# TensorE's background items of a fused convolution, attention and feed-forward stage, put at other steps of their quads

## The chip, the cores and the metric

The kernel runs on one core of one Trainium2 chip. The metric is the device time in microseconds (us). A core has four compute engines with a queue of instructions each: TensorE (PE in the profile; its weight loads are PEld), VectorE (DVE), ScalarE (ACT) and GpSimd (POOL); SyncE (SP) issues DMAs. Engines wait for one another by semaphores. TensorE writes PSUM, eight banks of 2 KB a partition, and the others read it.

## The reference

Four images of 128 channels and 64x64 pixels go through a group norm and a 3x3 deformable convolution (layer 0), then as 4096 tokens an image through attention and two feed-forward parts (layer 1). Cut to what matters:

```
x = x + deform_conv(group_norm(x))                 # 9 taps, bilinear corners gathered by offset
t = tokens(x)
q = ring(layer_norm(t).reshape(.., 16 heads, 8) + theta)     # products of cosines
attn = softmax(q q^T / sqrt(8)) q                  # 1024 tokens by 1024, 16 heads, 8 wide
x1 = ln(t_n + attn @ w_comb.T + b)
t = t + ln(x1 + relu(cos(x1[:8]) cos(ry) @ w1.T + b1) @ w2.T + b2)
t = t + experts(layer_norm(t))                     # gate logits, softmax over tokens, top 8 of them
```

The attention takes the tokens of an image as one sequence of 4096 here (the reference's shapes follow from its input), with the scores symmetric in the two token indices.

## The kernel before

The program has four stages: offsets, the convolution of the first image, a main stage (`stage_main`), and experts. The change is in the main stage alone.

**Quads and steps.** The main stage works on 16 quads, a quad being four heads of one image (`QUADRUPLES`, numbered 0 to 15 here). A quad has 8 units of 512 query tokens, and 304 steps (`Plan.steps`). A step is three slabs of 128 by 512 scores. For each step k TensorE computes the scores (L1157, three matmuls), ScalarE takes the exponential of 128x1536 numbers at once (L1255), and later TensorE multiplies the result with the values, a group of four heads at a time (L1189, 8 records of 512 columns). Because scores are symmetric, one part of the exponentials is kept (`e_kept`), turned by 16 DMAs and four VectorE transposes (L1140, L1151) and used as `e_turned` (L1180, 16 records, a group too). 256 groups of values a quad, 32 a unit.

**TensorE's order.** `AttnStep.quad_pe` writes it out step by step (k from 2 to 305). In step k it waits until the exponential of step k - 2 is done, because there are two PSUM tiles of scores; issues the scores of step k; then so many value groups; then the background item that is placed at k, if there is one. How many groups:

```
at_once = total if over else 0 if k in background else 1
needed = max(background[k][0] if k in background else 0, plan.before.get(k - 1, 0))
... range(min(max(min(ready - done, at_once), ready - done - self.PV_BEHIND, needed - done), closed - done))
```

So a step has one group, or none where an item stands; but where more than `PV_BEHIND` = 2 ready groups wait, or where a buffer of exponentials has to come free (`plan.before`: ScalarE's exponential k waits for them), the groups are caught up in that step, item or not. Items placed at step 306 or later are issued one behind the other at the quad's end, ahead of the next quad's step 2.

**Background items.** They are the rest of TensorE's work, in a fixed order a quad. All use one PSUM bank (`Misc`): an item waits until VectorE has read the one before it, and VectorE's program has the readers in the same order. Their names in this text:
- F0 to F7: `finish_pe` of the unit before (4 transposes of `acc_sb`, L1114). VectorE's read of the accumulators (L1092) comes ahead of it, and the next unit's first value group waits for that read too.
- tap: one of three products of a tile of the later images' convolution (`taps_pe`, L731), copied out at L740.
- gT, gL: the gate's transpose and logits (`gate_pe`, L1405, L1407). gT waits for two layer norms of VectorE (`norms_dve`), which wait for a load of `t1`.
- ctxT, comb, zbT, w1a, w1b, w2a, w2b: the seven items of a feed-forward pair (`item_pe`, L1511 to L1527). zbT reads what VectorE makes of comb in `first_dve` (L1447 to L1460); w1a and w1b are read by a relu (L1484), w2a and w2b together at L1490.
- stn0a to stn3b: transposes of the next quad's queries (`stage_pe`, L1054).

**Kinds of quads.** "conv first" (quad 0) and "conv" (1 to 3) have taps and no feed-forward, "conv ffn taps" (4 to 6) both, "conv ffn" (7 to 11) the feed-forward and the convolution's sampling on VectorE, "ffn six", "ffn choice" and "ffn" (12, 13, 14) the feed-forward alone, "last" (15). `PLACES` holds the steps of the items, a tuple for each kind.

**VectorE** runs `conv_quad`, `last_pair` and `ffn_quad`, where the readers of the items stand between the sampling of gathered pixels (L779 to L794), the transposes (L1151), the reads (L1092) and the norms. Where an item comes late, VectorE waits, and all behind it.

Of the kernel before, what the change touches and what calls it, by code (L numbers as in the profile page):

```python
# [1576 lines left out]
def stage_main(nc, d, r, stack):  # L1577
# [24 lines left out]
              (QUADRUPLES - 1, QUADRUPLES, "last", ()))  # L1602
    PLACES = {
        "conv first": (
            2, 4, 5, 6, 7, 26, 27, 46, 48, 49, 51, 52, 57, 59, 65, 67, 83, 88, 91, 98, 103, 111, 113, 120, 127, 139, 158, 161, 167,
            171, 176, 177, 180, 183, 184, 188, 198, 209, 214, 233, 236, 239, 244, 245, 251, 254, 256, 260, 261, 278, 298, 299,
        ),
        "conv": (
            2, 6, 7, 10, 13, 27, 28, 46, 52, 66, 82, 86, 88, 91, 99, 112, 114, 120, 126, 144, 157, 160, 163, 172, 176, 179, 180, 184,
            188, 190, 197, 211, 216, 233, 236, 238, 239, 245, 251, 252, 256, 257, 261, 276, 296, 301,  # L1610
        ),
        "conv ffn taps": (
# [3 lines left out]
        ),  # L1616
        "conv ffn": (
            5, 25, 28, 46, 49, 51, 53, 55, 66, 72, 77, 78, 82, 85, 106, 109, 121, 124, 128, 129, 132, 144, 149, 154, 155, 156, 159,
            181, 185, 194, 197, 199, 202, 203, 215, 221, 222, 227, 228, 234, 254, 259, 263, 270, 276, 294, 296, 300, 302, 303, 310,
            315,  # L1620
        ),
        "ffn six": (
# [3 lines left out]
        ),  # L1626
        "ffn choice": (
# [3 lines left out]
        ),  # L1631
        "ffn": (
# [3 lines left out]
        ),  # L1636
        "last": (
# [4 lines left out]
        ),  # L1642
    }
    SEGMENTS, at_misc, at_ffn, at_tap = [], 2, 0, TILES
# [1082 lines left out]
def build(nc, arrays, stages=("offsets", "conv", "main", "experts"), kinds={}):  # L2727
    d = Views(nc, arrays, kinds)
    with ExitStack() as whole:
        kept = Kept(nc, whole)  # L2730
        with ExitStack() as body:
            r = Shared(nc, body, kept)
            with ExitStack() as front:
                r.idx = front.enter_context(nc.sbuf_tensor("idx", [P, IMAGES * TILES * TAPS], I32))
                if "offsets" in stages:
                    with ExitStack() as st:
                        stage_offsets(nc, d, r, st)
                if "conv" in stages:
                    with ExitStack() as st:
                        stage_conv_first(nc, d, r, st)  # L2740
            if "main" in stages:
                with ExitStack() as st:
                    stage_main(nc, d, r, st)
        if "experts" in stages:
            with ExitStack() as st:
                stage_experts(nc, d, kept, st)
# [11 lines left out]
```

## Time and profile before

| | us |
|---|---|
| three timed runs | 7758.5, 7771.48, 7775.35; median 7771.48 |
| profiled execution, span | 7878.3 |
| ScalarE's exponentials, first to last start in the profile | 780.4 to 7622.4 |

The profiled execution took 107 us more than the median of the timed runs. Its span is the time from the first to the last instruction. In the profile a quad is the stretch between two exponentials 304 apart; the first exponentials of quads 1 to 15 start at 1253.0, 1677.4, 2098.7, 2516.9, 2946.8, 3382.2, 3816.2, 4242.6, 4668.4, 5091.3, 5512.3, 5934.1, 6354.2, 6775.6 and 7188.8 us. Step k of quad q is found by counting exponentials (L1255) from there.

### The profile page before, as it was taken

The page shows a single profiled execution, that of the slowest core. Times are in us where ns is not written, and L with a number is a line of the kernel's source. Part 1 is how long each engine was busy: PE and PEld are TensorE (multiplying, and loading weights), DVE is VectorE, ACT ScalarE, POOL GpSimd, SP SyncE. Part 2 cuts the span into 40 slices and gives each one's busy share as a digit, 9 for nine tenths or more (in the row PEclk, how much of TensorE's full clock was granted, in tenths as well). Part 3 has the DMA queues.
Part 4 walks back from the last instruction along what each step waited for, and adds up shares of the span by engine and source line. Part 5 has one row for each costly group of instructions (what it writes and reads, how often), then busy time and mean ns, then how long its engine had stood idle before and what let it go on. Part 6 is the DMA issues. An engine that isn't in the chain of part 4 may idle for free. (4 is left out here: it accounts for less than half of the span.)

```text
span 7878.3 us, 154169 instructions
## 1 busy us (share of the span) xinstructions
PE 6921.9 (88%) x58691; PEld 1859.1 (24%) x58691; DVE 4954.8 (63%) x12688; ACT 6811.0 (86%) x5455; POOL 1244.3 (16%) x1165
## 2 busy tenths in 40 slices
PE   4555799999999999999999999999999999999987
PEld 1444121111121222222221212222222212222224
DVE  5566555555555777777676767777775545454763
ACT  1222799999999999999999999999999999999971
POOL 1553111111111112111221111121210000000000
PEclk8777899999999999999999999999999999999997
DMA  6776575757566556656564545554643333232338
GB/s 214 208 210 185 125 167 138 171 137 166 141 159 147 147 135 169 154 131 157 124 144 112 138 115 132 120 136 113 145 117 77 98 74 92 69 98 64 99 98 265
DMA packets 1744564, 1080.93 MB, mean 137 GB/s; under 512 B 347914, under 2 KB 1645632, under 8 KB 1742828
## 3 DMA queue, kind: packets, MB, share of 16 engines
q1 hardware_dynamic: 1650972, 767.00, 40.2%
q0 software_dynamic: 92880, 304.42, 13.9%
q8 instruction: 448, 7.34, 0.4%
q14 instruction: 264, 2.16, 0.1%
HBM read 410.43 MB, written 190.83 MB: 76 GB/s over the span
## 5 line engine op out<-in xcount | busy, mean ns | idle before, releaser
L1255 ACT ACTIVATE e<-sc 128x1536 f32<-128x1536 f32 x4192 | 5715.2, 1604 | 193.2 <-PE sc L1157 121.7
L1189 PE MATMUL acc<-e,v_cur 128*9 128x512 f32 x25152 | 3341.7, 599 | 45.5 <-DVE acc_sb L1092 44.4
L1157 PE MATMUL sc<-b_unit,a_cur 32*128 32x512 f16 x14592 | 1916.7, 388 | 358.3 <-ACT e L1255 277.2
L1157 PEld LDWEIGHTS sc<-b_unit,a_cur 32*128 32x128 f16 x14592 | 472.6, 91 | 3826.3 <-ACT e L1255 2890.3
L1151 DVE STREAM_TRANSPOSE e_turned<-e_turned 128x1024 f32<-128x1024 f32 x896 | 1060.7, 1221 | 147.9 <-DMA e_turned<-e_kept 114.8
L1255 ACT ACTIVATE e_kept<-sc 128x1536 f32<-128x1536 f32 x672 | 960.6, 1567 | 63.0 <-PE sc L1157 32.1
L757 POOL DMA_INDIRECT room<-taps,idx_st x432 | 520.4, 1205 | 2109.0 <-ACT e L1255 890.2
L757 POOL DMA_INDIRECT corners<-taps,idx_st x441 | 435.1, 987 | 2052.3 <-ACT e L1255 1563.5
L1189 PE MATMUL acc<-e_kept,v_cur 128*9 128x512 f32 x4032 | 715.0, 611 | 0.0
L1189 PEld LDWEIGHTS acc<-e,v_cur 128*9 128x9 f32 x25152 | 394.3, 88 | 797.9 <-issue 730.8
L1180 PE MATMUL acc<-e_turned,v_cur 128*9 128x256 f32 x7168 | 472.2, 381 | 0.0
L621 ACT COPY cf_val_t<-cf_ps_t 128x512 f32<-128x512 f32 (+1 forms) x96 | 43.8, 481 | 407.1 <-PE cf_ps_t L661 260.9
L512 POOL DMA_INDIRECT cf_corners<-table,cf_idx x288 | 288.5, 1002 | 422.8 <-DVE cf_idx L537 160.9
L1092 DVE COPY acc_sb<-acc 128x512 f32<-128x512 f32 x129 | 88.8, 689 | 423.4 <-PE acc L1189 423.4
L740 DVE COPY conv_vals<-misc 128x384 f32<-128x384 f32 x192 | 106.7, 556 | 286.9 <-PE misc L731 247.9
L779 DVE TENSOR_TENSOR corners<-corners,w_st 128x1536 f32<-128x1536 f32 x144 | 250.0, 1755 | 9.0 <-DVE f_xn L103 5.9
L779 DVE TENSOR_TENSOR room<-room,w_st 128x1536 f32<-128x1536 f32 x144 | 248.3, 1747 | 2.9 <-DVE ctx_t L1105 2.7
L1043 DVE COPY b_all<-misc 128x1024 f16<-128x1024 f16 x64 | 44.3, 692 | 291.5 <-PE misc L1054 287.0
L649 PE MATMUL cf_ps_tap<-dcnw,cf_columns 128*128 128x384 f32 x192 | 86.6, 597 | 154.8 <-DMA cf_columns<-x_norm 154.8
L1180 PEld LDWEIGHTS acc<-e_turned,v_cur 128*9 128x9 f32 x7168 | 152.2, 90 | 197.4 <-issue 98.4
L551 DVE SCALAR_TENSOR_TENSOR cf_val<-cf_corners,cf_w,cf_val 128x128 f32<-128x128 f32 x576 | 157.7, 346 | 45.8 <-remote 20.7
L731 PE MATMUL misc<-dcnw,columns 128*128 128x384 f32 x384 | 178.2, 546 | 8.3 <-DVE f_gx_t L1390 4.2
(421 smaller groups left out, 5222.5 us busy)
## 6 DMA issues: line engine op xcount, KB each, us to landing
e_turned<-e_kept SPq DMA_DIRECT2D x3584, 128.0 KB
taps<-conv_vals SPq DMA_DIRECT2D x256, 288.0 KB
taps<-cf_tapped SPq DMA_DIRECT2D x128, 288.0 KB
ew<-in_ew SPq DMA_DIRECT2D x12, 1024.0 KB, 7.8
ew<-in_ew SPq DMA_DIRECT2D x48, 256.0 KB, 6.8
x_ch<-in_x SPq DMA_DIRECT2D x4, 2048.0 KB, 12.6
qn<-q SPq DMA_DIRECT2D x64, 128.0 KB
ctx<-ctx_t SPq DMA_DIRECT2D x128, 64.0 KB
```

The source lines that it names most:

```text
L512: pool.indirect_dma_start(corners[j][:, k, :], None, d.table, bass.IndirectOffsetOnAxis(idx_st[j][:, k:k + 1], 0)).then_inc(gathered[j], 16)
L551: last = v.scalar_tensor_tensor(out=dst, in0=src, scalar=wt, in1=dst, op0=ALU.mult, op1=ALU.add)
L731: m.pe_give(self.nc.tensor.matmul(m.bank[:, 0:3 * P], self.columns[j % 2][:], self.r.dcnw[:, 3 * g:3 * g + 3, :].rearrange("p k c -> p (k ...
L740: m.dve_give(self.nc.vector.tensor_copy(self.tapped[j % 2][:, 3 * P * g:3 * P * (g + 1)], m.bank[:, 0:3 * P]))
L757: pool.indirect_dma_start(self.corners[s][:, k, :], None, self.d.tap_tables[min(n, PAIRS - 1) * 2 // TILES - 1], bass.IndirectOffsetOnAxis ...
L779: last = v.tensor_tensor(g[:, taps], g[:, taps], w, ALU.mult)
L1092: self.nc.vector.tensor_copy(dst, src).then_inc(self.acc_read, 1)
L1151: self.nc.vector.transpose(x, x).then_inc(self.half_turned, 1)
L1157: last = self.nc.tensor.matmul(self.sc[k % self.SC][:, i, :], self.a[rows, t * P:(t + 1) * P], self.bst[u % 2][rows, :], start=True, stop= ...
L1180: last = self.nc.tensor.matmul(dst[:, :, half, :], self.v[:, plan.tiles_of[g][bo % 2], h, :], lines[:, :, :, h, 32 * bo:32 * bo + 32], sta ...
L1189: last = self.nc.tensor.matmul(self.acc[32 * h:32 * h + self.E1, :], self.v[:, t, h, :], src, start=(i == 0), stop=(i == self.UNIT - 1))
L1255: self.nc.scalar.activation(out, self.sc[k % self.SC][:], ACT.Exp, scale=1.0 / HD ** 0.5).then_inc(self.exp_done, 1)
```

## The change

`PLACES` has other steps for seven of the eight kinds; "last" keeps its own. The number of items and their order are the same, so every engine but TensorE has the same program, and TensorE has the same instructions in another order: an item comes some steps earlier or later between scores and value groups, and because a step with an item holds no group unless groups have to be caught up, value groups move as well. Of the kinds that the text speaks of most:

```
--- before.py
+++ after.py
@@ -1602,43 +1602,45 @@
     PLACES = {
...
         "conv": (
-            2, 6, 7, 10, 13, 27, 28, 46, 52, 66, 82, 86, 88, 91, 99, 112, 114, 120, 126, 144, 157, 160, 163, 172, 176, 179, 180, 184,
-            188, 190, 197, 211, 216, 233, 236, 238, 239, 245, 251, 252, 256, 257, 261, 276, 296, 301,
+            3, 5, 7, 9, 11, 19, 23, 46, 50, 55, 83, 85, 89, 91, 93, 101, 105, 121, 126, 131, 158, 160, 164, 166, 168, 170, 172,
+            183, 185, 188, 196, 207, 212, 233, 235, 239, 241, 243, 245, 247, 255, 257, 260, 270, 298, 300,
         ),
         "conv ffn taps": (
-            6, 9, 10, 13, 23, 26, 28, 32, 38, 46, 49, 51, 52, 54, 67, 72, 73, 76, 79, 85, 89, 94, 96, 106, 109, 111, 112, 115, 122,
-            126, 127, 129, 131, 142, 150, 153, 154, 156, 157, 162, 168, 169, 182, 183, 184, 187, 188, 195, 200, 202, 204, 206, 216,
-            222, 223, 228, 231, 233, 239, 243, 244, 254, 257, 258, 259, 260, 267, 271, 275, 294, 296, 300, 302, 303, 306, 311,
+            7, 12, 14, 16, 26, 28, 30, 31, 34, 46, 48, 51, 53, 55, 65, 71, 74, 76, 77, 84, 86, 94, 96, 108, 110, 112, 113, 116,
+            124, 126, 133, 135, 137, 145, 151, 153, 156, 157, 160, 162, 170, 172, 184, 186, 188, 189, 192, 200, 202, 210, 212,
+            214, 221, 227, 229, 232, 233, 235, 238, 246, 248, 259, 261, 263, 264, 266, 267, 272, 274, 300, 302, 304, 306, 307,
+            308, 309,
         ),
         "conv ffn": (
-            5, 25, 28, 46, 49, 51, 53, 55, 66, 72, 77, 78, 82, 85, 106, 109, 121, 124, 128, 129, 132, 144, 149, 154, 155, 156, 159,
-            181, 185, 194, 197, 199, 202, 203, 215, 221, 222, 227, 228, 234, 254, 259, 263, 270, 276, 294, 296, 300, 302, 303, 310,
-            315,
+            7, 26, 28, 46, 48, 51, 53, 55, 65, 71, 74, 76, 77, 84, 108, 110, 122, 125, 127, 129, 131, 141, 147, 150, 152, 153,
+            159, 184, 186, 198, 200, 203, 205, 207, 217, 223, 226, 228, 229, 234, 256, 258, 260, 270, 272, 293, 295, 297, 299,
+            301, 303, 304,
         ),
...
         "ffn choice": (
-            2, 10, 12, 15, 16, 25, 26, 31, 35, 38, 56, 74, 76, 84, 88, 91, 92, 94, 105, 107, 108, 109, 110, 121, 122, 129, 130, 131,
-            139, 140, 141, 146, 147, 155, 157, 159, 161, 167, 168, 169, 180, 182, 185, 186, 187, 195, 217, 230, 233, 237, 240, 241,
-            243, 252, 253, 255, 259, 264, 276, 294, 298,
+            3, 10, 14, 15, 16, 22, 23, 26, 28, 29, 46, 72, 74, 83, 85, 91, 92, 94, 103, 104, 107, 109, 110, 121, 123, 129, 130,
+            131, 138, 139, 142, 144, 145, 153, 155, 159, 161, 167, 168, 169, 179, 180, 183, 185, 186, 196, 220, 222, 233, 235,
+            241, 242, 243, 253, 254, 257, 259, 260, 270, 293, 295,
         ),
...
```

"conv first" from step 158 on has the places of "conv" in nearly all items; "ffn six" and "ffn" are moved likewise, by 1 to 9 steps. Where steps of them are needed: in "ffn six" w2a and w2b stand at 36, 37, 70, 71, 112, 114, 183, 186, 221, 222, 261, 264 before and at 35, 36, 72, 73, 112, 113, 184, 185, 221, 222, 261, 262 after; in "ffn" ctxT, gT, gL, comb of the fourth pair stand at 161, 167, 168, 169 before and at 163, 169, 170, 171 after.

## Rows read from the trace of the kernel before

**Rows 1.** The page, part 1: busy us (share of the span), instructions.

```profile
PE 6921.9 (88%) x58691; PEld 1859.1 (24%) x58691; DVE 4954.8 (63%) x12688; ACT 6811.0 (86%) x5455; POOL 1244.3 (16%) x1165
```

**Rows 2.** Stretches: quads 3, 5, 14; busy us (instructions) by engine, PEclk, DMA.

```profile
core 0: us, PE busy (x) PEld busy (x) DVE busy (x) ACT busy (x) POOL busy (x), PEclk, DMA share, GB/s
2098.70:2516.90 418.20, 393.02 (x3359) 82.59 (x3351) 241.77 (x427) 412.07 (x306) 75.69 (x72) 1.00 0.63 153
2946.80:3382.20 435.40, 409.43 (x3460) 95.86 (x3456) 315.72 (x773) 412.44 (x306) 85.18 (x72) 0.98 0.61 147
6775.60:7188.80 413.20, 389.94 (x3444) 90.75 (x3440) 196.81 (x613) 409.34 (x306) 0.00 (x0) 1.00 0.33 82
```

**Rows 3.** Timeline (start, us, engine, line, operation, count), quad 5, TensorE.

```profile
3217.90 0.39 PE L1157 MATMUL sc<-b_unit,a_cur 32*128 32x512 f16 x3
3218.22 0.91 PE L731 MATMUL misc<-dcnw,columns 128*128 128x384 f32 x2
3219.07 0.39 PE L1157 MATMUL sc<-b_unit,a_cur 32*128 32x512 f16 x3
...
3221.53 1.04 PE L1189 MATMUL acc<-e,v_cur 128*9 128x512 f32 x8
3222.51 0.39 PE L1157 MATMUL sc<-b_unit,a_cur 32*128 32x512 f16 x3
```

**Rows 4.** Timeline, quad 14, step 161: three groups and ctxT; then ScalarE.

```profile
6993.23 0.39 PE L1157 MATMUL sc<-b_unit,a_cur 32*128 32x512 f16 x3
6993.55 2.76 PE L1189 MATMUL acc<-e,v_cur 128*9 128x512 f32 x24
6996.24 0.44 PE L1511 MATMUL misc<-ident,f_ctx 128*128 128x128 f32 x2
6996.61 0.39 PE L1157 MATMUL sc<-b_unit,a_cur 32*128 32x512 f16 x3
...
6991.48 4.27 ACT L1255 ACTIVATE e<-sc 128x1536 f32<-128x1536 f32 x3
6997.05 2.79 ACT L1255 ACTIVATE e<-sc 128x1536 f32<-128x1536 f32 x2 [1.30 <-PE sc L1157]
```

**Rows 5.** Timeline, quad 3, step 247: two groups; then ScalarE.

```profile
2435.78 1.90 PE L1189 MATMUL acc<-e,v_cur 128*9 128x512 f32 x16
...
2438.13 2.79 ACT L1255 ACTIVATE e<-sc 128x1536 f32<-128x1536 f32 x2 [0.32 <-PE sc L1157]
```

**Rows 6.** Timeline, quads 5 and 6, end of a quad: TensorE, ScalarE, VectorE.

```profile
3383.71 2.05 PE L1527 MATMUL misc<-w,conv_vals 128*128 128x128 f32 x16
...
3380.83 4.14 ACT L1255 ACTIVATE e<-sc 128x1536 f32<-128x1536 f32 x3 [1.49 <-PE acc L1189]
...
3377.46 0.69 DVE L1484 TENSOR_SCALAR conv_vals<-misc 128x512 f32<-128x512 f32 x1 [1.76 <-PE misc L1524]
3378.07 2.28 DVE L783 TENSOR_TENSOR corners<-corners 128x2048 f32<-128x2048 f32 x1
3380.38 0.69 DVE L1043 COPY b_all<-misc 128x1024 f16<-128x1024 f16 x1
```

**Rows 7.** Timeline, quad 5, VectorE from a tap's reader to the read.

```profile
3221.70 0.56 DVE L740 COPY conv_vals<-misc 128x384 f32<-128x384 f32 x1
...
3229.89 0.69 DVE L1092 COPY acc_sb<-acc 128x512 f32<-128x512 f32 x1 [1.02 <-PE acc L1189]
```

**Rows 8.** Timeline, quad 5: comb on TensorE, zbT's input on VectorE.

```profile
3136.28 0.71 PE L1514 MATMUL misc<-combw,f_ctx_t 128*128 128x128 f32 x4
...
3148.38 0.24 DVE L1460 CAST f_zb<-f_zr 128x18 bf16<-128x18 f32 x1
```

**Rows 9.** Timeline, quad 9, step 181: gT; then ScalarE.

```profile
4920.26 0.41 PE L1405 MATMUL misc<-ident,f_gx 128*128 128x128 f32 x2 [2.80 <-DVEq L1417]
...
4921.03 1.45 ACT L1255 ACTIVATE e_kept<-sc 128x1536 f32<-128x1536 f32 x1 [1.34 <-PE sc L1157]
4923.37 1.45 ACT L1255 ACTIVATE e<-sc 128x1536 f32<-128x1536 f32 x1 [0.89 <-PE sc L1157]
```

**Rows 10.** Stretches of 3.4 us around that gT, columns as in rows 2.

```profile
4917.70:4921.10 3.40, 0.84 (x9) 0.42 (x13) 2.97 (x11) 2.06 (x3) 1.90 (x2) 1.00 0.64 167
4921.10:4924.50 3.40, 3.40 (x19) 0.23 (x11) 3.40 (x4) 2.51 (x2) 1.23 (x1) 0.50 0.35 106
```

More of the change, by code:

```diff
@@ L1604, in stage_main @@
         "conv first": (
-            2, 4, 5, 6, 7, 26, 27, 46, 48, 49, 51, 52, 57, 59, 65, 67, 83, 88, 91, 98, 103, 111, 113, 120, 127, 139, 158, 161, 167,
-            171, 176, 177, 180, 183, 184, 188, 198, 209, 214, 233, 236, 239, 244, 245, 251, 254, 256, 260, 261, 278, 298, 299,
+            2, 6, 7, 10, 12, 22, 24, 46, 48, 51, 53, 55, 62, 64, 69, 70, 88, 91, 95, 97, 99, 108, 112, 121, 129, 134, 158, 160,
+            164, 166, 168, 170, 172, 183, 185, 188, 196, 207, 212, 233, 235, 239, 241, 243, 245, 247, 255, 257, 260, 270, 298,
+            300,
         ),
         "conv": (
-            2, 6, 7, 10, 13, 27, 28, 46, 52, 66, 82, 86, 88, 91, 99, 112, 114, 120, 126, 144, 157, 160, 163, 172, 176, 179, 180, 184,
-            188, 190, 197, 211, 216, 233, 236, 238, 239, 245, 251, 252, 256, 257, 261, 276, 296, 301,
+            3, 5, 7, 9, 11, 19, 23, 46, 50, 55, 83, 85, 89, 91, 93, 101, 105, 121, 126, 131, 158, 160, 164, 166, 168, 170, 172,
+            183, 185, 188, 196, 207, 212, 233, 235, 239, 241, 243, 245, 247, 255, 257, 260, 270, 298, 300,
         ),
         "conv ffn taps": (
[3 rows of a table removed]
[4 rows of a table added]
         ),
         "conv ffn": (
-            5, 25, 28, 46, 49, 51, 53, 55, 66, 72, 77, 78, 82, 85, 106, 109, 121, 124, 128, 129, 132, 144, 149, 154, 155, 156, 159,
-            181, 185, 194, 197, 199, 202, 203, 215, 221, 222, 227, 228, 234, 254, 259, 263, 270, 276, 294, 296, 300, 302, 303, 310,
-            315,
+            7, 26, 28, 46, 48, 51, 53, 55, 65, 71, 74, 76, 77, 84, 108, 110, 122, 125, 127, 129, 131, 141, 147, 150, 152, 153,
+            159, 184, 186, 198, 200, 203, 205, 207, 217, 223, 226, 228, 229, 234, 256, 258, 260, 270, 272, 293, 295, 297, 299,
+            301, 303, 304,
         ),
         "ffn six": (
[3 rows of a table removed]
[3 rows of a table added]
         ),
         "ffn choice": (
[3 rows of a table removed]
[3 rows of a table added]
         ),
         "ffn": (
[3 rows of a table removed]
[3 rows of a table added]
         ),
         "last": (
[4 rows of a table removed]
[4 rows of a table added]
         ),
```

20 rows, old and new, of the table PLACES are left out of this document.

## The prediction

> **What bounds the kernel now.** I read the busy shares first [rows 1]. They average over four stages, so the next view is the busy time by quad [rows 2]: in a quad of the convolution alone ScalarE is busy 412 of 418 us, with both kinds of items 412 of 435, in quad 14 409 of 413. ScalarE sets the pace, and TensorE is nearly as full: 393, 409 and 390 us. DMA and GpSimd have room. What ScalarE can't go below is its own pitch: three exponentials in a row behind a wait take 4.14 us where one takes 1.45 [rows 6, 9], so (4.14 - 1.45) / 2 = 1.345 us a step, 304 x 1.345 = 409 us a quad. Counted from the starts of the quads, quads 1 to 14 take 5936 us, 14 x 409 = 5724: some 210 us are waits. That is the purse. An item at a better step can give back a part of it and nothing more.
>
> The timelines give TensorE's cost of a step. Scores: 3217.90 to 3218.22, 0.32 us. A tap: 3218.22 to 3219.07, 0.85. A single group of values: 3221.53 to 3222.51, 0.98 [rows 3]. Three groups: 6993.55 to 6996.24, 2.69, so a group with another behind it takes some 0.86; two are recorded with 1.90, where a record is 0.07 longer than its hold on TensorE: 1.83. ctxT is 0.37 [rows 4, 5]. The same reading of other steps gives 0.57 for F and stn, 0.35 gT, 0.59 gL, 0.64 comb, about 0.33 zbT and w1, and 1.09 w2a or w2b (2.05 for the two [rows 6]). So scores and a group take 1.30, and a step gives TensorE back only 0.04 us: **what a crowded step loses is won back in steps without a group, hardly elsewhere.** An item with a group goes over by nearly its whole length.
>
> How much is free? TensorE issues the scores of step k + 2 just after exponential k ends, and exponential k + 2 has to start 1.45 us before its end is due. The rows say what is left: step 161 of quad 14 has 0.32 + 2.69 + 0.37 = 3.38, 2.04 over the pitch, and ScalarE, whose record before ended at 6995.75, ends the next at 6998.50, 1.40 late: 0.64 was free [rows 4]. I take **0.7 us free, once, until an emptier step refills it**. Forced groups are worse: where a buffer has to come free, the groups that exponential k waits for are issued in step k + 1, and ScalarE stands 1.49 us [rows 6].
>
> **The change part by part.** It adds no work. I walked the loop of the diff's kernel and laid out each step's scores, groups and item, before and after, with these lengths. Only places that differ are told.
>
> *Conv (quads 1 to 3, and quad 0 from step 158).* Taps stand at every other step (158 to 172, 235 to 247), so groups pile up and are caught up together with an item. Step 172 has three groups and a tap: 0.32 + 2.69 + 0.85 = 3.86, 2.5 over; the 0.7 is already used by the group and tap of 168, so some 2.3 us are lost against 0.36 before (one group and a tap). Step 247: two groups and a tap, 1.7 over and nothing free, against two groups alone, 0.32 idle [rows 5]: +1.2. Five more steps with two groups (60, 87, 135, 209, 236) at 0.3 make +1.5; less 0.6, since the last places of taps and F are cleaner. A quad: 1.9 + 1.2 + 1.5 - 0.6 = 4.0; four quads **+16**.
>
> *Conv ffn taps (quads 4 to 6)*, four terms.
> (a) The end. Before, w2a and w2b stand past step 305; now w1b, stn3b, w2a, w2b (306 to 309) do, and TensorE can issue nothing else between them. They share the bank, so each waits for VectorE: relu of w1b 0.43 + 0.69, then VectorE has a sampling sum of 2.28 ahead of the copy of stn3b, 0.69, and only then w2a [rows 6]: 0.43 + 0.69 + 2.28 + 0.69 + 2.2 = 6.3 us against 2.2. +4.1; the read of the accumulators stands behind them on VectorE and the first groups wait for it, +2.2; three forced groups of step 304 become fewer, -1.3. **+5.0.**
> (b) Late reads. The tap at 188 goes to 192 and that at 115 to 116. From a tap's reader to the read that follows, VectorE has 3229.89 - 1.02 - 3221.70 = 7.2 us (the rest of a sampling, four transposes); before, it had 1.02 to spare [rows 7]. Four steps later is 5.4 us later: about 4 late, some 3.6 felt at 197, and about 1.9 at 122. **+5.5.**
> (c) zbT nearer to comb. From comb's start to the end of VectorE's last input for zbT are 3148.62 - 3136.28 = 12.3 us, 9.2 steps [rows 8]. The distance was 11 (131 to 142) and 10 (206 to 216); it is 8 (137 to 145) and 7 (214 to 221). TensorE stands 2.3 and 3.1 us; less the 0.7 and what the missing group leaves, 1.4 + 1.8 = **+3.2.**
> (d) Catch-ups: steps 161, 236 and 273 get three groups (1.1 to 1.2 each), 157 w2b with a group, 248 and 267 a tap with one, 232 to 234 four items' work; gone are two groups before a waiting F4 (2.0) and the pair 183, 184 behind a late gT. **+4.7.**
> Sum 18.4 a quad, three quads **+55**.
>
> *Conv ffn (7 to 11).* Here waits do go. gT at 181 stands 2.80 us for VectorE's norms, which wait for a load; ScalarE loses 1.34 [rows 9]. It moves to 184, those at 25 and 254 to 26 and 256: -2.1. F5 and what follows, 194 to 198: -0.8. Nothing is left past step 304: -1.6. Against it: 293 to 303 alternate, so two forced catch-ups (299, 303) and small ones replace one of 303, +1.9; w2b with a group at 77, 153, 229, +1.7; three groups at 209, 210: +0.5; F4's neighbourhood +0.8. Five quads at 0.4: **+2**. Norms are served by the same load as before, so this cover holds.
>
> *Ffn six* **+2.7**: w2a and w2b with a group each, one behind the other (72, 73; 184, 185), 1.06 each, and 0.6 of others. *Ffn choice* **+5.5**: zbT 6 and 7 steps behind comb (22, 138; 9 and 8 before), 2.4 and 1.8; w2a and w2b at 28, 29 and 144, 145, 1.4 each; less 1.3 for stn2a at 217, that was late, and 0.2. *Ffn* **+3.4**: three groups at 172 instead of two (+0.9), w2b with a group at 148, 188 and 260, +1.5, two groups at 87, +0.8, others.
>
> 16 + 55 + 2 + 11.6 = **+85 us**.
>
> **TensorE's clock.** After the wait of 2.80 us the granted clock is 0.50 for 3.4 us (1.2 of 2.4 GHz); TensorE was busy 0.84 of the 3.4 us before [rows 10], and ScalarE loses 0.89 in one step there beyond the wait's own 1.34, and 0.4 in the next [rows 9]. A low stretch costs 1.3. I count 17 new waits of 1.5 us and more (five in each quad 4 to 6, two in 13), and about 9 low stretches that should go: 8 x 1.3 = **+10**. The Trainium skill (TensorE: Matmul & The Clock Gate, HAM oscillation) prices throttled time at half its length: 1.7 us for such a stretch, +14 instead of +10. That the same page wants waits between bursts avoided speaks against these places.
>
> The sum is +95 against the profiled execution of 7878.3, whose span is 107 us over the timed median; its waits are the same program's, so I carry the difference over: 7771.5 + 95 = **7866 us**.
>
> **Bounds.** Not shown before is a tap behind three groups; by [rows 4, 5] it lies between 1.3 and 2.5 us. The free 0.7 may be 0.5 or 0.9 and moves about 60 crowded places by 0.2: 12 us either way. VectorE's chains may be shorter by what it waited within them, which bounds (b) and (c) from nothing to +10 a quad. Below nothing: all gains and no loss, next part.
>
> **Rivals.**
> *Only TensorE's own crowding counts*, and VectorE makes up its lateness, since it is busy only 316 of 435 us [rows 2]: (a), (b), (c) 3 x 13.7 and choice 4.2 go, and the clock's 10: +40, **7811**. Against it: the read has 1.02 to spare, not 5. 0.17.
> *Faster*: the places were late before and crowding is absorbed, because the two score tiles cover more than 0.7. Then what counts is the waits taken away: gT of five quads with its low clock 13, forced ends of eight quads at 2.0 16, the pair 183, 184 with what follows in three quads 14, F4 6, F5 5: -54, **7717**. It decides if three groups in a step cost ScalarE under 0.3; [rows 4] say 1.40. 0.10.
> *The clock doubles it*: alternate items leave steps with neither group nor item (20 instead of 13 in conv), and low stretches come there too, some 30 at 1.3: +134, **7905**. For: TensorE's busy share falls in just these stretches. 0.15.
> *Nothing moves*: gains and losses cancel within 0.2% (16 us), which is what a measurement of this kernel can tell from no change. 0.05.
> The forecast has 0.53, with its own range 7840 to 7890.
>
> **Range and chances.** 7790 to 7915 leaves out the two last small cases and the tails. Faster 0.10, same 0.05, slower 0.85.
>
> **What would show it.** In the trace after: ScalarE idle about 2.3 us at step 172 of quads 1 to 3, with 24 records of L1189 and a tap ahead; over 4 us at the start of quads 5, 6 and 7; 3 us at 196 of quads 4 to 6 behind L1092; no wait of gT at 184 in quads 7 to 11, whose length stays within 3 us; quads 4 to 6 longer by 15 to 22 each. If quads 4 to 6 are not longer, the prediction is wrong.

## The result, and the profile after

| | us |
|---|---|
| kernel before, four timed runs | 7758.5 to 7775.35, median 7772.89 |
| changed kernel, four timed runs | 7844.57 to 7855.14, median 7850.42 |
| ratio | 1.0104, 95% interval 1.0089 to 1.0118: 81 us slower (69 to 92) |
| forecast | 7866, +95; range 7790 to 7915 |

The changed kernel is slower, as forecast, by somewhat less. (The two medians by themselves differ by 77.5 us.) Its profiled execution took 7855.1 us, near its median. That of before had taken 107 us too long, so I profiled the kernel before a second time ("before, second profile": 7771.8 us). Of the excess 75.6 us lay ahead of the first exponential and 34 in the main stage, 14 of them in quad 0. The comparisons below are with the second profile.

The page after, span and part 1, against [rows 1]: the same work, the same busy time.

```profile
span 7853.3 us, 154169 instructions
PE 6928.4 (88%) x58691; PEld 1848.9 (24%) x58691; DVE 4957.1 (63%) x12688; ACT 6812.2 (87%) x5455; POOL 1241.8 (16%) x1165
```

The stretches that answer to [rows 2], quads 3, 5 and 14 after:

```profile
2006.70:2425.90 419.20, 393.08 (x3359) 83.53 (x3351) 241.74 (x427) 411.95 (x307) 71.39 (x72) 1.00 0.63 153
2866.80:3316.50 449.70, 410.80 (x3460) 95.74 (x3456) 315.87 (x772) 413.25 (x306) 84.91 (x72) 0.98 0.58 142
6745.50:7162.60 417.10, 391.32 (x3447) 91.59 (x3440) 196.54 (x613) 410.21 (x306) 0.00 (x0) 1.00 0.33 81
```

Quad 5 went from 435.4 us [rows 2] (433.4 in the second profile) to 449.7 with the busy times unchanged: waits. By kind, changed kernel minus second profile of before, counted from exponential 0 to exponential 0 of the next quad: quads 0 to 3 -0.3, 2.3, 1.7, 1.1; quads 4 to 7 **12.9, 16.3, 17.8, 14.1**; quads 8 to 11 1.0, 3.7, -1.6, 1.9; quads 12 to 14 1.4, 6.2, 1.6; "last" 2.6, though its places are the same. Quads whose places were not touched mostly move by up to 3 us between two profiles, some by 4 to 4.5, and quads 0 and 1 of the two profiles of before by 13.6 and 5.9. So only sums and waits that repeat in every quad are read below.

ScalarE's own waits by what ended them. First the kernel before (second profile), then the changed one: us, times.

```profile
  PE sc L1157: 185.2, 224
  DMA e_turned<-e_kept: 32.9, 15
  PE acc L1189: 30.4, 35
```

```profile
  PE sc L1157: 245.0, 270
  PE acc L1189: 39.8, 43
  DMA e_turned<-e_kept: 35.9, 10
```

46 more waits and 60 us more for the scores, 8 more waits and 9 us more for buffers (ended by value groups), 3 us more for DMAs in fewer waits.

**A crowded step.** Conv, quad 3, step 172 after: three groups (L1189, 2240.93 to 2243.63; the line shown holds 19 of their 24 records), then a tap (L731), then the scores that ScalarE needs.

```profile
2240.61 0.39 PE L1157 MATMUL sc<-b_unit,a_cur 32*128 32x512 f16 x3
2241.38 2.32 PE L1189 MATMUL acc<-e,v_cur 128*9 128x512 f32 x19
2243.63 0.91 PE L731 MATMUL misc<-dcnw,columns 128*128 128x384 f32 x2
2244.47 0.39 PE L1157 MATMUL sc<-b_unit,a_cur 32*128 32x512 f16 x3
2244.99 2.79 ACT L1255 ACTIVATE e<-sc 128x1536 f32<-128x1536 f32 x2 [2.15 <-PE sc L1157]
```

From scores to scores 3.86 us, the forecast's sum to the digit. Counted between starts of exponentials over 1.331 us (the distance of two starts where nothing waits), which is how all numbers "at step k" below are meant, 2.29 us are lost at 173 in each of quads 1, 2 and 3; forecast 2.3. At 248 it is 1.62, forecast 1.7.

**The end of a quad of conv ffn taps.** Quad 5 after, TensorE and VectorE past step 305, then ScalarE:

```profile
3319.05 0.39 PE L1524 MATMUL misc<-f_zf_t,w 54*128 54x256 bf16 x2
3320.09 2.28 DVE L783 TENSOR_TENSOR corners<-corners 128x2048 f32<-128x2048 f32 x1
3320.23 0.62 PE L1054 MATMUL misc<-ident,wb 128*128 128x128 f16 x8 [0.79 <-DVE conv_vals L1484]
3322.40 0.69 DVE L1043 COPY b_all<-misc 128x1024 f16<-128x1024 f16 x1
3323.15 3.79 PE L1527 MATMUL misc<-w,conv_vals 128*128 128x128 f32 x16 [2.30 <-DVE b_all L1043]
3327.60 1.45 ACT L1255 ACTIVATE e<-sc 128x1536 f32<-128x1536 f32 x1 [7.88 <-PE sc L1157]
```

The chain is the forecast's: w1b, its relu, stn3b, the sampling sum of 2.28 ahead of its copy, w2a and w2b. Its last link is longer than in the sum: w2a and w2b take 3.79 us, where the same pair took 2.05 [rows 6]. From w1b to the next scores are 3326.86 - 3319.05 = 7.8 us, for 6.3 in the sum. The stretches around the pair show why (columns as in [rows 2]):

```profile
3318.73:3322.14 3.41, 1.33 (x14) 0.56 (x10) 2.66 (x2) 0.99 (x1) 0.00 (x0) 1.00 0.00 0
3322.14:3325.55 3.41, 2.40 (x11) 2.41 (x12) 3.27 (x5) 0.00 (x0) 0.00 (x0) 0.50 0.00 0
3325.55:3328.97 3.42, 2.35 (x13) 1.22 (x12) 3.16 (x9) 1.37 (x2) 0.00 (x0) 0.50 0.07 7
```

TensorE was busy 1.33 of 3.41 us. From 3322.14 on, while it waits for VectorE, the granted clock is 0.50, the 1.2 GHz level, and it stays there for 10.24 us, to 3332.38. The whole pair runs in this time, and it lost 1.74 us. (By the Trainium skill, TensorE: Matmul & The Clock Gate, HAM oscillation, throttled time costs half its length. For the pair's 3.79 us that makes 1.9, an estimate from that page; the trace agrees, with 1.74, where TensorE is busy throughout.)

**A late read.** Quad 5 after, from the tap at 192 on (a copy, sums left out, four transposes, the read), then the group and the exponential:

```profile
3150.89 0.56 DVE L740 COPY conv_vals<-misc 128x384 f32<-128x384 f32 x1 [0.63 <-PE misc L731]
3153.43 4.62 DVE L1151 STREAM_TRANSPOSE e_turned<-e_turned 128x1024 f32<-128x1024 f32 x4
3157.98 0.65 DVE L1092 COPY acc_sb<-acc 128x512 f32<-128x512 f32 x1
3158.68 1.89 PE L1189 MATMUL acc<-e,v_cur 128*9 128x512 f32 x8 [3.68 <-DVE acc_sb L1092]
3161.16 1.45 ACT L1255 ACTIVATE e<-sc 128x1536 f32<-128x1536 f32 x1 [4.19 <-PE sc L1157]
```

VectorE runs from the copy to the read without a wait for TensorE, 3157.98 - 3150.89 = 7.1 us (forecast 7.2). TensorE waits 3.68, and then its group takes 1.8 where one takes 0.98: the granted clock is 0.50 from 3158.30 to 3161.71.

### The profile page after: what moved, and what is told of

It reads as the page before. It is cut to its first block and busy times, and to the rows that moved or that the text cites. A ratio compares the mean times of both kernels' runs of the same rounds, so it can differ in the third digit from the quotient of the medians.

```text
span 7853.3 us, 154169 instructions
## 1 busy us (share of the span) xinstructions
PE 6928.4 (88%) x58691; PEld 1848.9 (24%) x58691; DVE 4957.1 (63%) x12688; ACT 6812.2 (87%) x5455; POOL 1241.8 (16%) x1165
## 3 DMA queue, kind: packets, MB, share of 16 engines
q14 instruction: 265, 2.16, 0.1%
## 5 line engine op out<-in xcount | busy, mean ns | idle before, releaser
L1189 PE MATMUL acc<-e,v_cur 128*9 128x512 f32 x25152 | 3357.6, 603 | 83.5 <-DVE acc_sb L1092 83.5
L1189 PE MATMUL acc<-e_kept,v_cur 128*9 128x512 f32 x4032 | 712.8, 607 | 0.0
L1189 PEld LDWEIGHTS acc<-e,v_cur 128*9 128x9 f32 x25152 | 400.7, 89 | 856.3 <-issue 738.9
L1092 DVE COPY acc_sb<-acc 128x512 f32<-128x512 f32 x129 | 88.5, 686 | 702.1 <-PE acc L1189 701.8
L731 PE MATMUL misc<-dcnw,columns 128*128 128x384 f32 x384 | 176.7, 542 | 3.5 <-DVE ctx_t L1105 3.5
L661 PE MATMUL cf_ps_t<-ident,cf_val 128*128 128x128 f32 x1152 | 142.1, 285 | 13.2 <-DVE cf_val L551 7.3
```

What stands on the lines that cost most here:

```text
L661: last = nc.tensor.matmul(ps_t[at % 2][:, (k - g0) * P:(k - g0 + 1) * P], val[j % 2][c][:, k, :], r.ident[:], start=(c == 0), stop=(c == 1))
L731: m.pe_give(self.nc.tensor.matmul(m.bank[:, 0:3 * P], self.columns[j % 2][:], self.r.dcnw[:, 3 * g:3 * g + 3, :].rearrange("p k c -> p (k ...
L1189: last = self.nc.tensor.matmul(self.acc[32 * h:32 * h + self.E1, :], self.v[:, t, h, :], src, start=(i == 0), stop=(i == self.UNIT - 1))
```

## The experiments

Five runs ask where the time is: the second profile, and four kernels with the change in one group of kinds at a time. The kernel before was timed anew beside each group of runs, with medians of 7774.5, 7768.2 and 7771.2 us (7772.9 beside the changed kernel). The ratios go by these; plain times from two groups can be some 5 us apart for that reason alone.

**Kernel before, profiled again.**

> The kernel before, unchanged, for a second profile. The profile of before that the prediction used took 7878.3 us, 107 over the median of its timed runs. Of these, 73 us lie ahead of the first exponential (780.4 us there, 707.7 in the profile after). The rest should then be waits of the main stage that don't belong to the program: quad 0 is 13.9 us and quad 1 3.5 us longer in that profile than in the one after. Theory A (such waits are noise of one execution): the second profile is near 7780 us, its quads 0 to 3 together are some 20 us shorter than in the first (1736), and its stalls of 3.1 and 3.6 us at steps 112 and 206 of quad 1 are gone. Theory B (the waits are caused by the places): the quads repeat within 1 us each, and the new places of conv then save time, against the forecast of +4.0 a quad.

Measured: 7771.8 us. Quads 0 to 3 together 1713.2 us, 23 less than in the first profile; the stalls at 112 and 206 of quad 1 are gone, and others stand at 127, 200 and 216 (3.67, 1.35, 1.73). Theory A.

**Conv ffn taps alone.** Only the tuple `"conv ffn taps"` of the diff.

> The new places for conv ffn taps (quads 4 to 6) alone. Theory A, the prediction's sum: 18.4 us a quad and five new low stretches of TensorE's clock in each (1.3 each), 55 to 75 us in all; the profiles show the cost at the starts of quads 5, 6 and 7 (over 4 us each), at step 197 (4), at 122 (2) and behind zbT at 145 and 221. About +60, 7832 us, ratio 1.0077. Theory B, only TensorE's own crowding counts and VectorE makes up its lateness: 3 x 4.7 = +14 us, ratio 1.0018, with no stalls at the places named. Theory C, the other kinds carry the difference: under 1.001.

Measured: 1.0059 (1.0044 to 1.0073), +46 us (34 to 57). Quads 4 to 7 are longer by 12.4, 17.1, 20.3 and 7.8 in its profile, with the stalls at the named places. Over half of the change's loss, and Theory B (+14) is out. Of Theory A the places hold; its 55 to 75 us only touch the interval, so the size is smaller.

**Conv first and conv alone.**

> The new places for conv first and conv (quads 0 to 3) alone. Theory A, the prediction's sum: four times 4.0 = +16 us, ratio 1.0021, with 2.3 us at step 173 (behind three groups and a tap at 172) and 1.6 at 248. Theory B, what the two profiles suggest by their quads 1 to 3 (-3.5, -1.9 and +1.0 us): nothing or a gain, -5 us, ratio 0.9994, because other waits go with it that the walk did not have; then the profile must show which stalls of before are gone in every one of quads 1 to 3.

Measured: 1.0006 (0.9997 to 1.0015), +5 us (-2 to 12). The 2.29 at 173 and 1.62 at 248 are there in each quad, yet the kinds cost a third of the forecast: A's +16 and B's -5 both lie outside the interval. What of before is gone, in each of quads 1 to 3: (second profile) 0.34, 0.34, 0.34 at 191; 1.35, 1.48, 1.16 at 200; 1.73, 0.33, 0.06 at 216; 0.47 at 253, 0.60 at 258. At 200 of quad 2 it is a wait for the transposed exponentials, which the walk priced at nothing; in the changed kernel no exponential of that stretch waits. Kernel before, second profile, then changed:

```profile
1858.59 2.79 ACT L1255 ACTIVATE e_kept<-sc 128x1536 f32<-128x1536 f32 x2 [1.29 <-DMA e_turned<-e_kept]
```

```profile
1859.11 5.67 ACT L1255 ACTIVATE e<-sc 128x1536 f32<-128x1536 f32 x4
1864.45 3.02 ACT L1255 ACTIVATE e_kept<-sc 128x1536 f32<-128x1536 f32 x2
```

The profiles of all runs bear this out for most of them: in the seven with the old conv places a wait stands at 200 in every one of quads 1 to 3 (0.1 to 2.2 us), in the five with the new places in none, and 253 and 258 go likewise. Not so at 216, where two of the five have 0.7 to 1.6 again. So that the waits at 200, 253 and 258 go with the conv places is shown; that those at 200 go by way of the taps' stores, which stand ahead of these loads in SP's queue and come two steps earlier now (190 to 188), is argued only.

**Conv ffn alone.**

> The new places for conv ffn (quads 7 to 11) alone. Theory A, the prediction's sum: gains (gT at 181, F5 at 194, the end past step 304) and losses (299, 303, w2b with a group) cancel but for 0.4 us a quad, +2 us, ratio 1.0003. Theory B: F5 moved from 194 to 198 is late, since it is the transposes after a read that the next unit's groups wait for; the profile after has a stall of 1.5 to 2.4 us at step 196 or 197 that my sum did not hold, and a second low stretch behind 299: +2 us a quad, +10 in all, ratio 1.0013. In both the stall behind gT at 182 is gone. The rise of 10.2 us in quad 7 of the profile after is the end of quad 6 and must be absent here.

Measured: 1.0011 (1.0001 to 1.0020), +8 us (1 to 16). gT's stall at 182 is gone, and 1.3 to 3.1 us stand at 196 in quads 8 to 11, where before there was at most 0.5 at 195; 1.91 at 299 and 1.61 at 303 in all. The stalls are Theory B's; the time alone does not decide, as both +2 and +10 are in the interval, and the profiled execution was the fastest of the eleven (7764.4 us) and shows no loss over quads 8 to 11. Quad 7 begins with 1.37 and 0.55 at steps 2 and 4, as in before, so the rise at its start does belong to the end of quad 6; its 6.2 us over the second profile are 2.3 over the first, with a wait of 2.93 for a transfer at step 20.

**The three kinds of ffn alone.**

> The new places for ffn six, ffn choice and ffn (quads 12 to 14) alone: what is left of the change beside the three kinds tried. Theory A, the forecast's sum: 2.7 + 5.5 + 3.4 = 11.6 us, ratio 1.0015. Theory B, what the profiles of the changed kernel and of the second profile of before say (+1.4, +6.2, +1.6): 9 us, ratio 1.0012. The four parts should then add up to the change's 77 us: 46 + 5 + 8 + 12 = 71.

Measured: 1.0012 (1.0003 to 1.0021), +9 us (2 to 16); both theories are inside. The four parts give 46 + 5 + 8 + 9 = 68, the change 81 (69 to 92): they add up within their intervals, and nothing asks for a term between kinds, though one of some 10 us would not be seen.

The next four take single terms.

**The end of conv ffn taps put back**, in the changed kernel:

```diff
-            ..., 272, 274, 300, 302, 304, 306, 307, 308, 309,
+            ..., 272, 274, 294, 296, 300, 302, 303, 306, 311,
```

> The changed kernel, with the last seven places of conv ffn taps (zbT to w2b of the fourth pair: 300, 302, 304, 306, 307, 308, 309) put back to 294, 296, 300, 302, 303, 306, 311. Theory A, the forecast's term (a) has the right mechanism but was too small: the profiles show 9 to 10 us more than before at steps 1 to 6 of quads 5, 6 and 7, and 1.3 less at 303; all of it goes, 3 x 8 = 24 us, 7827 us. Theory B, the forecast's own size: 3 x 5.0 = 15 us, 7835 us. Theory C, the work only moves (the same four items have to be done by someone): the stalls at the quads' starts are replaced by others before step 304, under 5 us, 7847 us.

Measured: 7830.8 us, 1.0080 (1.0065 to 1.0096), 20 us less than the changed kernel's 7850.4, and 15 less if each is set against the kernel before timed beside it (62.6 for 77.5). That is B's size or somewhat more; A's 24 is still in the interval, C is out. In its profile the pair is at full clock again, and the quad starts 1.37 late, no longer 6 to 8:

```profile
3305.42 4.14 ACT L1255 ACTIVATE e<-sc 128x1536 f32<-128x1536 f32 x3 [1.49 <-PE acc L1189]
3308.30 2.05 PE L1527 MATMUL misc<-w,conv_vals 128*128 128x128 f32 x16
3310.80 1.45 ACT L1255 ACTIVATE e<-sc 128x1536 f32<-128x1536 f32 x1 [1.24 <-PE sc L1157]
```

**The items ahead of the two reads earlier**, in the changed kernel:

```diff
-  113, 116, ... 184, 186, 188, 189, 192, 200,
+  113, 115, ... 184, 185, 186, 187, 188, 200,
```

> The changed kernel, with the taps and gL ahead of two reads of the accumulators earlier in conv ffn taps: tap 116 to 115, and 186, 188, 189, 192 to 185, 186, 187, 188; F3 and F5 stay. VectorE then reaches the reads of steps 121 and 196 in time. Theory A, term (b) is a local cost: the stalls at 122 (2.1 to 3.2 us) and 197 to 199 (5 to 6 us) of quads 4 to 6 go and nothing comes, 3 x 8 = 24 us, 7826 us. Theory B, the forecast's size, 3 x 5.5 = 16 us. Theory C, part of it is given back: four items at four steps running wait for VectorE's copies, so ScalarE loses some 1.7 us at 189 and 0.7 at 116, and what is left is 3 x 2.5 = 7 us, 7843 us.

Measured: 7835.3 us, 1.0084 (1.0069 to 1.0100), 15 us less, or 10 against the kernels before timed beside them (67.1 for 77.5); quads 4 to 6 are 8.4, 6.0 and 5.3 shorter in the profile. The stalls at 197 are gone and those at 122 are 0.4 to 0.7; in their place stand 1.78 at 189 and 0.71 at 116. Quad 5, the tap that waits for VectorE's copy of the item before it, and ScalarE behind it:

```profile
3140.38 0.91 PE L731 MATMUL misc<-dcnw,columns 128*128 128x384 f32 x2 [0.82 <-DVE conv_vals L740]
3141.75 2.79 ACT L1255 ACTIVATE e<-sc 128x1536 f32<-128x1536 f32 x2 [1.66 <-PE sc L1157]
```

8.1 - 2.5 = 5.6 a quad by these stalls, 17 in all: A's size less C's payback. The timed 10 to 15 lie between C's 7 and B's 16. The interval reaches from some 3 to 27 us and excludes none of the three; it is the profile that shows C's payback.

**Four items a little later**, in the changed kernel:

```diff
 "conv"
-  170, 172, 183, ... 245, 247, 255,
+  170, 173, 183, ... 245, 248, 255,
 "conv ffn taps"
-  137, 145, 151, ... 214, 221, 227,
+  137, 148, 151, ... 214, 224, 227,
```

> The changed kernel, with four items one or three steps later: in conv the tap at 172 (behind three groups) to 173 and the one at 247 (behind two) to 248; in conv ffn taps zbT at 145 to 148 and at 221 to 224, so that it is 11 and 10 steps behind comb, as before. Theory A, each of these places is a loss of its own, as the forecast has it: 2.3 us at 173 falls to 1.4 and 1.6 at 248 to 0.8, three or four times 1.7, and zbT's waits go, 3 x 3.2: -16 us, 7834 us. Theory B, the stretch is full, not the step: ScalarE loses the same at the next step (0.8 at 174 and 249), and w1a, w1b and w2b behind zbT now meet groups that were caught up earlier: 0 us, 7850 us.

Measured: 7844.4 us, 1.0106 (1.0091 to 1.0122): 6 us less by the medians, 1 against the kernels before timed beside them, and a ratio no lower than the change's 1.0104. Theory B. In quad 3 the tap stands alone behind the scores now, and ScalarE waits twice:

```profile
2234.25 2.32 PE L1189 MATMUL acc<-e,v_cur 128*9 128x512 f32 x19
2236.51 0.39 PE L1157 MATMUL sc<-b_unit,a_cur 32*128 32x512 f16 x3
2237.02 1.45 ACT L1255 ACTIVATE e<-sc 128x1536 f32<-128x1536 f32 x1 [1.30 <-PE sc L1157]
2237.81 0.91 PE L731 MATMUL misc<-dcnw,columns 128*128 128x384 f32 x2
2239.17 2.79 ACT L1255 ACTIVATE e<-sc 128x1536 f32<-128x1536 f32 x2 [0.70 <-PE sc L1157]
```

1.45 + 0.82 for 2.29, and 0.78 + 0.74 for 1.62, in all three quads. zbT's waits (1.3 to 1.5 at 146 with 1.0 behind, 1.9 to 2.1 at 222 with 1.0 behind) go, and 0.6 to 1.1 come at 152, 0.9 to 1.4 at 228, 0.5 more at 158 and at 234: in two of three quads 4 to 6 shorter by 3.8, in quad 5 longer by 6.5, with twelve low stretches of the clock where the changed kernel has six.

**gT of conv ffn later**, in the kernel before:

```diff
-  5, 25, 28, ... 159, 181, 185, 194, ... 234, 254, 259,
+  5, 26, 28, ... 159, 184, 185, 194, ... 234, 256, 259,
```

> The kernel before, with gT of conv ffn later: 25, 181, 254 to 26, 184, 256, as in the change. Theory A, the forecast's term: the waits at 182 and 255 go, 2.1 us a quad and the clock's share of 1.0 behind 182, 5 x 3.1 = 15 us, ratio 0.9980. Theory B, the chain behind gT on VectorE comes later too, so that the read of the accumulators at 195 is late by some 2 us (it was 0.5): half is given back, 5 x 1.3 = 6 us, ratio 0.9992.

Measured: 0.9994 (0.9985 to 1.0003), -5 us (-12 to 2): Theory B, and A only just outside. The stall at 182 (1.2 to 2.7 with up to 1.1 behind) is nowhere, and all five quads have 2.6 to 3.0 at 195 and 0.7 to 1.0 at 196, where 0.4 to 0.5 was. Quad 9 of it:

```profile
4823.16 0.65 DVE L1092 COPY acc_sb<-acc 128x512 f32<-128x512 f32 x1
4823.95 0.63 PE L1114 MATMUL misc<-ident,acc_sb 128*128 128x128 f32 x4 [3.24 <-DVE acc_sb L1092]
4825.03 1.45 ACT L1255 ACTIVATE e<-sc 128x1536 f32<-128x1536 f32 x1 [2.08 <-PE sc L1157]
4827.29 1.45 ACT L1255 ACTIVATE e<-sc 128x1536 f32<-128x1536 f32 x1 [0.81 <-PE sc L1157]
```

VectorE does gT's copy, a sampling and four transposes and then the read. Move its first link by three steps and the last comes late. The changed kernel moved F5 from 194 to 198 and so behind the read, but the next unit's groups wait for the same read: quad 9 there, gT without a wait, then the same stall at 196.

```profile
4878.47 0.44 PE L1405 MATMUL misc<-ident,f_gx 128*128 128x128 f32 x2
...
4895.23 1.51 PE L1189 MATMUL acc<-e,v_cur 128*9 128x512 f32 x8 [1.92 <-DVE acc_sb L1092]
4897.41 1.45 ACT L1255 ACTIVATE e<-sc 128x1536 f32<-128x1536 f32 x1 [1.86 <-PE sc L1157]
```

The last two look for a version that is better than both.

**The last items of eight quads earlier**, in the kernel before:

```diff
 "conv ffn"
-  294, 296, 300, 302, 303, 310, 315,
+  292, 293, 294, 295, 297, 302, 310,
 "conv ffn taps"
-  294, 296, 300, 302, 303, 306, 311,
+  292, 294, 295, 296, 297, 302, 304,
```

> The kernel before, with the last seven places of conv ffn (294, 296, 300, 302, 303, 310, 315 to 292, 293, 294, 295, 297, 302, 310) and of conv ffn taps (294, 296, 300, 302, 303, 306, 311 to 292, 294, 295, 296, 297, 302, 304). Exponential 303 waits for groups that can only be caught up where no item stands. Theory A: the stall of 1.9 to 2.2 us at 303 falls below 0.5 in eight quads, and 0.5 comes at 295 and 299 in its place: 1.1 a quad, 9 us, ratio 0.9989. Theory B: the forecast's rival priced these forced ends at 2.0 a quad: 16 us, ratio 0.9979. Theory C: it only moves, 0.

Measured: 0.9993 (0.9983 to 1.0002), -5 us (-13 to 2). At 303 2.14 to 2.18 fell to 0.35 in quads 8 to 11; at 295 and 296 came 3.6, 1.0, 2.4 and 1.0 together (five items in six steps; the third, stn3a, waits 0.60 for VectorE's relu in quad 8). The two large ones are the quads in which the granted clock is 0.50 there, and in 9 and 11 it is not. B's 16 is out, A's 9 and C's 0 are both in the interval; by the profile most of it moved.

**Places chosen by the walk for six kinds**, in the kernel before. Of conv ffn:

```diff
-  5, 25, 28, 46, ... 154, 155, 156, 159, 181, 185, 194, 197, 199, 202, 203, 215, 221, 222, 227, 228, 234, 254, 259, 263, 270,
-  276, 294, 296, 300, 302, 303, 310, 315,
+  3, 28, 34, 46, ... 151, 152, 156, 162, 183, 186, 195, 198, 202, 204, 206, 218, 220, 226, 227, 229, 238, 257, 259, 262, 269,
+  276, 292, 293, 294, 295, 297, 302, 310,
```

> A version meant to beat both: the places of six kinds (all but conv first and last) chosen anew by the step walk of the forecast, with what the runs so far showed: an item no earlier than VectorE can serve it (gT of conv ffn at 183 or 184, with F5 right behind the read that then comes late), w1a to w2b of the last pair before the forced groups of 303, no three groups beside an item, zbT no nearer to comb. Theory A, waits are what the purse of 210 us holds, and the walk sees them: conv ffn 4 us a quad, taps 3, six 3.7, choice 2.6, conv 1.3, ffn 1: 5 x 4 + 3 x 3 + 3.7 + 2.6 + 4 + 1 = 40 us, ratio 0.9948, with no stall over 1.2 us at 182 and 303 in quads 7 to 11. Theory B, before is already at the edge, and each wait taken away comes back behind the next item (as the read at 195 did when gT alone was moved): within 10 us, ratio 0.9987 or more. Theory C: slower, if the waits for DMAs grow because VectorE's reads and transposes come at other times.

Measured: 7734.1 us, **0.9955 (0.9941 to 0.9968), -35 us (25 to 46)**: Theory A, a version faster than both. ScalarE's waits in its profile, against 185.2 and 245.0 above:

```profile
  PE sc L1157: 145.0, 156
  PE acc L1189: 40.0, 54
  DMA e_turned<-e_kept: 29.2, 16
```

Quads 4 to 6 are 6.6, 7.0 and 7.2 shorter than in the second profile of before, quads 8 to 11 4.3, 2.9, 7.3 and -0.2. No stall is left at 182; F4's step costs 0.19 at 160 for 0.85, and gT at 183 with F5 at 195 leaves 0.8 to 1.0 at 196 of quads 8 to 11 (2.2 in quad 7). 0.9 to 3.3 at 295 is new in quads 7 to 11, and the clock is at 0.50 near there in seven of quads 4 to 11. Of conv ffn taps, 2.11 at 158 (two groups before a waiting F4) and 1.8 to 3.3 at 185 to 187 are gone; 1.4 to 2.0 at 296 and 1.8 at 204 of two quads are new. Not all of it is gain: quad 7 is 3.9 longer, and quad 13 (ffn choice), for which 2.6 were expected, is 9.4 longer in this one execution, with eight low stretches of the clock for one and 3.6 at step 11. In the whole stage there are 50 stretches at half clock for 54.

## Why the prediction was right, and where it was off

The direction, the main cause (quads 4 to 7) and TensorE's arithmetic hold. The steps, by their own numbers:

- *ScalarE's pitch.* 1.345 us was read from two steps right behind a wait. Over 62 steps in a row without a wait (quads 1 and 2 of before, 1632.14 to 1714.77) the starts are 1.333 apart, over two rows of 58 that begin in quads 13 and 14 they are 1.331 and 1.332. So 304 steps take 405 us and not 409, and the purse of quads 1 to 14 was some 270 us, not 210: 5935.8 - 14 x 304 x 1.331. In the second profile it is 251, in the changed kernel 331, in the version by the walk 210. No term of the forecast hangs on it beyond some 0.01 us a step.
- *TensorE's cost of a step and the 0.7 us free.* Right: 2.29 for 2.3, 1.62 for 1.7, 3.86 for 3.86.
- *Conv, +16.* +5 (-2 to 12). The two crowded steps were right; what failed is "less 0.6, since the last places of taps and F are cleaner". Cleaner was worth some 3 us a quad: the waits at 191 and 200, perhaps 216, and those at 253 and 258. The walk of before saw no loss at 200 and 216, where ScalarE waits for transposed exponentials.
- *Conv ffn taps, +55 without the clock.* Timed +46 (34 to 57); 61 in the two profiles with the clock in it, by quads 4 to 7, against 55 + 15 stretches x 1.3 = 75. Term (a) was too small: steps 1 to 6 of quads 5 to 7 have 11.2, 10.2 and 11.0 against 1.9 before, less 1.3 at 303, 7.6 for 5.0; putting the end back gave 15 to 20 us, 5 to 6.7 a quad. (b): 2.9 at 122 and 123 plus 5.2 at 197 to 199 make 8.1 for 5.5, but putting the items back returned only 10 to 15 us in all, since they then wait for VectorE. (c): 6.0 for 3.2, and the shift of zbT alone got none of it back for certain. Of the excess, 8.0 a quad in all, 4.9 bear the mark of the low clock, which I had booked apart: 1.7 in w2a and w2b, and 1.0 to 1.1 each behind the stalls of 146, 197 and 222. What is left of the 20.4 a quad, (d), is -1.3 instead of +4.7: the waits of before at 24 and 25, 158, and 184 to 190 were worth more than I had seen. Set with its clock beside it (five stretches of 1.3), (a) to (c) were forecast at 20.2 a quad and came to 21.7; what was mis-sized in this kind is (d), by 6.0 a quad.
- *Conv ffn, +2.* +8 (1 to 16). The failing step is "gT ... moves to 184 ...: -2.1. F5 and what follows, 194 to 198: -0.8" with no term for the read behind them: 1.3 to 3.1 at 196. I had worked out just such a chain for the taps, and not looked for it here.
- *Ffn six, choice, ffn, +11.6.* +9 (2 to 16).
- *Clock, +10.* "I count 17 new waits ... and about 9 low stretches that should go." By the trace's records of the granted clock, the main stage has 184.6 and 184.8 us at half clock in the two profiles of before and 231.9 after: 54, 54 and 68 stretches of 3.4 us. Quads 4 to 6 went from 14 to 20, quad 7 from 2 to 6, the last four from 5 to 11; in quads 8 to 11, where some should go, there are 14 in both, since the stall only moved from gT to the read. So 14 more, not 8, at 1.0 of ScalarE's time each (1.04 at 147 and 223, behind a stall; and quad 15, whose places are the same in all, takes 436.2 to 436.6 us up to its last exponential in the four profiles where it has five low stretches and 432.6 to 433.6 in five of the six where it has two): some +14 by this estimate, for +10. The number of stretches was too low and the price of 1.3 too high. That leaves about 65 for all other terms, where the forecast had 85.
- *The sum.* That 95 came as near to 81 as it did owes something to luck: by these parts conv was 11 us too dear and (d) 18, against 6 too little for conv ffn and some 5 for (a) to (c).
- *Carrying +95 over to the median.* Sound, but its premise, "its waits are the same program's", was false for 34 us of the main stage.

The rivals: crowding alone (+40) fails on the stalls at 122, 146, 197 and 222 and on the end put back; it would have needed VectorE to make up its lateness, which it does not do within a chain. By the time, too, +40 and +134 lie outside 69 to 92. The clock doubling (+134) had some 30 stretches more than the forecast's 8; there are 14. Faster and nothing fail on the ratio. What was to show it did: 2.3 at 173, over 4 at the starts of quads 5, 6 and 7 (6.1 to 8.0 at step 2 alone), 3.8 to 4.4 at 197 behind L1092, no wait of gT at 184. Two signs were wrong, and both because the cost of an end falls into the quad behind it: quads 4 to 6 were to be "longer by 15 to 22 each", and quad 4 is only 12.9; the length of quads 7 to 11 was to stay "within 3 us", and quad 7 is 14.1 longer (quad 9 3.7).

## What to carry to other kernels

Where two engines are both nearly full, the place of a background item is a time for a chain and not for a step: price from the moved item to the last thing behind it on the other engine (here a copy, a sampling, four transposes, a read) before booking a removed wait as a gain; with gT later, 3.8 us a quad of waits at 182 to 184 and 255 to 257 went and 3.4 came back at the read, and the timed gain is 1 (-0.4 to 2.4). An overfull stretch loses its excess wherever the item in it stands (2.29 or 1.45 + 0.82), so a single item is worth moving only to where there is room, and items that share a buffer must not be queued last with nothing between them. Profile the kernel before twice: one execution had 34 us of waits in the stage that the next had not.

## What the runs showed of the hardware

- Behind 3.41 us in which TensorE was busy 1.33, its clock was 0.50 for 10.24 us, and a pair of products that takes 2.05 us took 3.79. Behind 3.41 us with 0.11 busy (quad 5 after, ahead of the late group) it was 0.50 for 3.41. It also fell where TensorE had only short waits of 0.63 us, busy 2.16 of 3.42 (quad 9, second profile of before, at 4866.17); a group there took 1.90. In the middle of a quad the same shows as a second, smaller stall one step behind the first: 1.40 then 1.04 at 146 and 147, 2.13 then 1.03 at 222 and 223.
- Two executions of one program both had 54 such stretches in the main stage, but single quads differ by up to three (quad 10 has 1 and 4). A term for the clock can be read from the sum over a stage, hardly from one quad. In quad 15, the same in all kernels, three low stretches more go with some 3 us more.
- Stalls that come of order alone repeat to 0.01 us from quad to quad and from kernel to kernel (2.29 at 173 in six quads of two kernels), while those that end on a transfer do not (0.1 to 3.4 us at step 20 of quads 5 to 7, over all profiles but the first). The first kind can be added up beforehand. The second kind and the low stretches are what differs between profiles of one program; how much of the scatter of a quad is due to each was not worked out.
